# One normalisation a step earlier, its epsilon added column by column: a change to VectorE's order in a four-layer attention block

## The chip, the cores and the metric

One core of one Trainium2 chip runs the program. The time is the device time of one launch in microseconds, the median of three runs. The trace is one profiled execution of the same program, taken apart from those runs.

## The reference, cut to what matters

A batch of 16 sequences of 128 tokens with 128 features goes through four layers of cross attention and feed-forward, and then through one gated block of self attention and mixture of experts. The change touches the four layers alone.

```python
def _norm(x):
    m = jnp.mean(x, axis=-1, keepdims=True)
    s = jnp.sqrt(jnp.mean((x - m) ** 2, axis=-1, keepdims=True))
    return (x - m) / (s + EPS)                  # EPS = 1e-6, added to the root

def _attention(x, src, dist, bias, Wq, Wk, Wv, Wo, Wth, bth, Wto, bto):   # 16 heads of 64
    q = einsum('bfd,dnh->bfnh', x, Wq) * H ** (-0.5)
    k, v = einsum('btd,dnh->btnh', src, Wk), einsum('btd,dnh->btnh', src, Wv)
    hbias = relu(dist[..., None] @ Wth + bth)   # 32 values for each pair of positions
    qs_bias = (hbias @ Wto + bto)[..., 0]
    logits = einsum('btnh,bfnh->bnft', k, q) + bias + qs_bias[:, None]
    out = einsum('bnft,btnh->bfnh', softmax(logits), v)
    return einsum('bfnh,nhd->bfd', out, Wo)

for i in range(4):
    x = x + _attention(_norm(x), ctx, dist, mask, Wq[i], ...)     # first norm
    x = x + relu(_norm(x) @ Wf1[i] + bf1[i]) @ Wf2[i] + bf2[i]    # second norm
```

## The kernel before, in words

All data are float32 and stay in SBUF. One batch of one layer is a *unit*; there are 64 units, and unit u is batch u mod 16 of layer u div 16. A software pipeline goes through steps i = 0 to 63 (with -1 and 64 at the edges). In step i TensorE computes scores of unit i, applies the probabilities of unit i-1 and projects them out, makes keys, values and queries of unit i+1, the first feed-forward matmul of unit i-1 and the second of unit i-2. Each engine has its own hand-written order for a step, with semaphores between the engines; nothing reorders it at run time.

A unit is normalised twice: before its queries (half `a`, buffer half 0) and before its feed-forward (half `b`, half 1). Before the change, step i treats the *pair* of unit i+1's `a` and unit i-1's `b`. The way of such a pair is:

- VectorE: `residual1` (line 929) adds the projected attention of unit i-1; `stats` (881) and `moments` (886) make mean and variance of both halves.
- GpSimd: `root` (1317) raises both variances to 0.5 in one instruction, `sd`, a tile of 128x2.
- VectorE: `inverse_deviation` adds epsilon to both columns (891, `sde`) and takes the reciprocal (893, `rs`); `normalise` (900) writes `hh`, 128x128, once for `a` and once for `b`.
- TensorE: `turn_pair` transposes the two halves of `hh` (480 for `a`, 483 for `b`) into one PSUM bank; VectorE's `keep_pair` (909) copies both to `hhT`.
- TensorE: queries (427 on `hhT`) of unit i+1 and first feed-forward matmul (504) of unit i-1, after which ScalarE keeps the queries (709) and VectorE the hidden layer (942, `hid`).

TensorE's `turn_pair` stands behind the transposes of the first two quarters of the probabilities (406) and ahead of keys, queries and feed-forward of the step.

The bias of the scores, 32 relu terms for each of four units, is work that is spread over the steps as filler. ScalarE makes 22 relus (682), VectorE weighs and adds them (844; the first term of a group is 841) in PSUM, GpSimd makes the other ten terms with three instructions each on 128x512 (1333, 1340, 1352). `Z_PLAN`, `TERM_PLAN` and `POOL_PLAN` say how many go at each place of a step, by i mod 4; `more(q)` in VectorE's step runs the q-th entry of its plan. In the step that is 3 mod 4, VectorE ends with the sum of the two parts (852). GpSimd also multiplies the exponentials by the reciprocal sums (`norm`, 1321), four times a step, the third right behind `root`.

The stretch after the four layers (the gated block) has its own order. Its first pieces for two batches, `f_first` in 12 parts, run inside steps 61 and 62 at the places of `more`.

Of the kernel before, what the change touches and what calls it, by code (L numbers as in the profile page):

```python
# [8 lines left out]
ALU = mybir.AluOpType  # L9
# [33 lines left out]
TERM_PLAN = ((1, 1, 3, 1), (1, 1, 3, 1), (1, 1, 2, 1), (1, 1, 2, 1))  # L43
# [7 lines left out]
F_FIRST_PARTS = ((0, 1), (2, 3, 4, 5, 6), (7, 8, 9), (10, 11))  # L51
# [13 lines left out]
def wait(eng, sem, value):  # L65

    if value < 1:
        return
    eng.wait_ge(sem, value)
# [30 lines left out]
def block_program(nc, x, ctx_in, dist, mask, g_xattn, g_ffn, Wq, Wk, Wv, Wo, Wth, bth, Wto, bto,  # L100
                  Wf1, bf1, Wf2, bf2, W_qkv, b_qkv, W_gate, b_gate, W_experts, b_experts, out):
    with ExitStack() as stack:
# [3 lines left out]
        def sem(name):  # L106
            return stack.enter_context(nc.semaphore(name))
# [123 lines left out]
        bna, bnb, vara, varb, rooted, sdeps, rstd = [sem(n) for n in ("bna", "bnb", "vara", "varb", "rooted", "sdeps", "rstd")]  # L231
# [21 lines left out]
        def there(u):  # L253
            return 0 <= u < UNITS
# [4 lines left out]
        def pairs(i):  # L259

            return i + 2

        def halves(i):

            return slice(0 if there(i + 1) else 1, 2 if there(i - 1) else 1)

# [555 lines left out]
        def _(dve):  # L822
# [43 lines left out]
            def inverse(u, c):  # L866
                dve.wait_ge(exp_done, upto(u, 4, c))
                wait(dve, normed, upto(u - 1, 4, c))
                vec.reciprocal(rinv[:, c, :], rsum[:, c, :]).then_inc(inv_done, 1)  # L869

            def stats(u, a):

                s, b = u % 2, u % BATCHES
                if a == 1:
                    dve.wait_ge(resid1, upto(u))
                elif u < BATCHES:
                    dve.wait_ge(ln_done, b + 1)
                else:
                    dve.wait_ge(resid2, upto(u - BATCHES))
                wait(dve, hb_done if a else ha_done, upto(u - 2))  # L880
                vec.bn_stats(st[:, s, a, :], x_all[:, b, :]).then_inc(bnb if a else bna, 1)  # L881

            def moments(u, a):
                s = u % 2
                dve.wait_ge(bnb if a else bna, upto(u))
                vec.bn_aggr(mv[:, s, a, :], st[:, s, a, :]).then_inc(varb if a else vara, 1)

            def inverse_deviation(i):
                s, h = (i + 1) % 2, halves(i)
                dve.wait_ge(rooted, pairs(i))  # L890
                vec.tensor_scalar(sde[:, s, h], sd[:, s, h], NORM_EPS, None, ALU.add).then_inc(sdeps, 1)  # L891
                dve.wait_ge(sdeps, pairs(i))
                vec.reciprocal(rs[:, s, h], sde[:, s, h]).then_inc(rstd, 1)

            def normalise(u, a):
                s, b = u % 2, u % BATCHES
                i = u + 1 if a else u - 1
                dve.wait_ge(rstd, pairs(i))
                wait(dve, hh_done, pairs(i - 2))
                vec.tensor_scalar(hh[:, s, a, :], x_all[:, b, :], mv[:, s, a, 0:1], rs[:, s, a:a + 1],  # L900
                                  ALU.subtract, ALU.mult).then_inc(hb_done if a else ha_done, 1)
# [29 lines left out]
            def residual2(u):  # L931
                dve.wait_ge(f2_done, upto(u))
                dve.wait_ge(xb_done, upto(u))
                vec.tensor_tensor(x_all[:, u % BATCHES, :], FF_BANK[:, 0:P], xb[:, u % 2, :], ALU.add).then_inc(resid2, 1)
# [16 lines left out]
            def step(i):  # L951
# [3 lines left out]
                def more(q):  # L955

                    if i in F_EARLY:
                        for part in F_FIRST_PARTS[q]:
                            f_first(0, F_EARLY.index(i), part)
                    elif cur:  # L960
                        terms(plan[q])
# [13 lines left out]
                if cur:  # L975
                    inverse(i, 1)
                if prev:
                    residual1(i - 1)
                if nxt:
                    stats(i + 1, 0)  # L980
                if prev:
                    stats(i - 1, 1)
                if nxt:
                    moments(i + 1, 0)
                if prev:
                    moments(i - 1, 1)
                if cur:
                    inverse(i, 2)
                inverse_deviation(i)
                if nxt:  # L990
                    normalise(i + 1, 0)
                if prev:
                    normalise(i - 1, 1)
                more(1)
                if old:
                    residual2(i - 2)
                keep_pair(i)
# [8 lines left out]
                more(2)  # L1006
                if prev:
                    hidden(i - 1)
                more(3)
# [256 lines left out]
            stats(0, 0)  # L1266
            moments(0, 0)
            terms(2)
            keep_keys(0, 0)
            inverse_deviation(-1)  # L1270
            normalise(0, 0)
            terms(2)
            keep_pair(-1)
# [28 lines left out]
        def _(pool):  # L1302
# [7 lines left out]
            def root(i):  # L1310
                s, h = (i + 1) % 2, halves(i)
                if there(i + 1):
                    pool.wait_ge(vara, upto(i + 1))
                if there(i - 1):
                    pool.wait_ge(varb, upto(i - 1))
                wait(pool, sdeps, pairs(i - 2))
                gp.tensor_tensor(sd[:, s, h], mv[:, s, h, 1], half[:, 0:h.stop - h.start], ALU.pow).then_inc(rooted, 1)  # L1317
# [113 lines left out]
            ops(3)  # L1431
            root(-1)
# [31 lines left out]
```

## Time and profile before

| | |
|---|---|
| median of three runs | 1273.55 us (1273.51 to 1273.87) |
| profiled execution: its time | 1273.89 us |
| profiled execution: its span, first to last instruction | 1272.1 us |
| mean granted TensorE clock | 0.988 of full speed (2.4 GHz) |
| busy: TensorE matmul, VectorE, ScalarE, GpSimd | 91%, 87%, 84%, 63% of the span |

The first scores begin 38.4 us into the span and the last step's at 1075.9 us, so that the 64 steps are most of the time. Line numbers are those of the kernel before. In a timeline, a bracket shows how long the engine had been idle before the instruction, and which instruction ended that wait.

### The profile page before, as it was taken

What the parts mean: (1) busy time and instruction counts of PE and PEld (TensorE: products, weight loads), DVE (VectorE), ACT (ScalarE), POOL (GpSimd) and SP (SyncE); (2) the same over time, 40 slices, a digit from 0 to 9 for tenths busy, and PEclk for the clock granted to TensorE, in tenths of its full rate; (3) what the DMA queues carried; (4) which work ended last, traced back from release to release, by engine and by line L of the source; (5) the groups of instructions that cost most, each with busy time, mean ns of one, the idle gap of its engine ahead of it and who ended that gap; (6) DMA issues with size and microseconds to landing.
All of it is one profiled execution on the core that took longest, in us unless ns stands there. A gap on an engine that the chain in (4) does not pass through costs nothing.

```text
span 1272.1 us, 35758 instructions
## 1 busy us (share of the span) xinstructions
PE 1155.1 (91%) x11216; PEld 989.3 (78%) x11216; DVE 1103.9 (87%) x4455; ACT 1070.1 (84%) x3387; POOL 804.0 (63%) x917
## 2 busy tenths in 40 slices
PE   1499999999999999999999999999999999899897
PEld 1478888888888888888888888888888888666665
DVE  4988888888988888889898989898989887599996
ACT  4698888888888888888898888888888876588886
POOL 5577777777777777777777777777777733211110
PEclk9799999999999999999999999999999999899999
DMA  7400000001100000011000000000000000000000
GB/s 221 117 2 2 2 2 2 2 2 53 32 2 2 2 2 2 2 51 35 2 2 2 2 2 2 2 2 2 2 2 2 2 2 2 1 7 9 9 9 10
DMA packets 21147, 19.29 MB, mean 15 GB/s; under 512 B 5848, under 2 KB 17504, under 8 KB 20960
## 3 DMA queue, kind: packets, MB, share of 16 engines
q1 hardware_dynamic: 20960, 17.00, 4.5%
q8 instruction: 92, 1.51, 0.5%
q14 instruction: 95, 0.78, 0.2%
HBM read 15.95 MB, written 1.05 MB: 13 GB/s over the span
## 4 chain that ended last, share of the span: by engine, by line
PE 57%; DVE 25%; issue 8%; POOL 4%; ACT 3%; SPq 1%; DMA 1%; DVEq 0%; POOLq 0%; ACTq 0%
PE B L427 13%; PE B L392 10%; PE B L420 9%; PE B L469 9%; DVE B L844 6%; DVE sde L891 5%; DVE hh L900 4%; POOL sd L1317 3%; PE B L567 3%; PE B L406 2%; PE B L504 2%; ACT prob L753 2%; PE B L579 2%; PE B L646 2%; DVE st L881 2%
## 5 line engine op out<-in xcount | busy, mean ns | idle before, releaser
L1321 POOL TENSOR_TENSOR prob<-prob,rinv 128x512 f32<-128x512 f32 x256 | 266.6, 1041 | 266.8 <-DVE rinv L869 264.4
L692 ACT ACTIVATE prob<-score,nmax 128x128 f32<-128x128 f32 x1024 | 395.4, 390 | 9.6 <-DVE nmax L861 7.5
L682 ACT ACTIVATE relu_z<-dist_all,cst_all 128x512 f32<-128x512 f32 x356 | 276.6, 811 | 12.1 <-DMA dist_all<-in_fside_BxSxS 10.5
L861 DVE CUSTOM_DVE_ANT_0 score<-B,bias 128x128 f32<-128x128 f32 x1024 | 225.0, 284 | 42.8 <-PE B L392 42.7
L844 DVE SCALAR_TENSOR_TENSOR B<-relu_z,cst_all,B 128x512 f32<-128x512 f32 x340 | 254.4, 748 | 6.8 <-ACT relu_z L682 2.6
L692 ACT ACTIVATION_READ_ACCUMULATOR prob<-score,nmax 128x1 f32 x1024 | 194.4, 190 | 0.0
L709 ACT ACTIVATE qT<-B 128x512 f32<-128x512 f32 x128 | 76.7, 599 | 128.1 <-PE B L427 128.1
L1352 POOL TENSOR_TENSOR pool_acc<-pool_acc,clamped 128x512 f32<-128x512 f32 x140 | 178.3, 1273 | 6.7
L427 PE MATMUL B<-ctxT_all,wk 128*128 128x128 f32 x1024 | 143.5, 284 | 14.8 <-DVE nmax L861 14.1
L427 PEld LDWEIGHTS B<-ctxT_all,wk 128*128 128x128 f32 x1024 | 129.4, 197 | 25.8 <-DVE nmax L861 14.3
L406 PEld LDWEIGHTS B<-ident,prob 128*128 128x128 f32 x1024 | 120.2, 141 | 35.6 <-issue 33.4
L699 ACT ACTIVATE probT<-B 128x512 f32<-128x512 f32 x256 | 141.7, 592 | 3.7 <-PE B L406 3.6
L427 PE MATMUL B<-hhT,wq 128*128 128x128 f32 x1024 | 142.4, 283 | 1.8 <-DVE hhT L909 0.9
L406 PE MATMUL B<-ident,prob 128*128 128x128 f32 x1024 | 143.1, 273 | 0.6 <-POOL prob L1321 0.6
L392 PE MATMUL B<-kT,qT 64*128 64x128 f32 x2048 | 131.5, 278 | 11.3 <-DVE hid L942 10.5
L392 PEld LDWEIGHTS B<-kT,qT 64*128 64x128 f32 x2048 | 120.2, 188 | 23.2 <-issue 23.2
L427 PEld LDWEIGHTS B<-hhT,wq 128*128 128x128 f32 x1024 | 125.6, 193 | 11.4 <-DVE hhT L909 10.7
L449 PE MATMUL B<-wv,ctxT_all 128*128 128x512 f32 x256 | 131.5, 596 | 0.0
L1340 POOL TENSOR_SCALAR clamped<-clamp_in,cst_all 128x512 f32<-128x512 f32 x156 | 123.0, 788 | 11.0
L1333 POOL TENSOR_SCALAR clamp_in<-dist_all,cst_all 128x512 f32<-128x512 f32 x156 | 121.6, 779 | 9.5 <-DVE cst_all L1244 9.5
L469 PE MATMUL B<-wo,oT 128*128 128x128 f32 x1024 | 125.2, 275 | 1.8 <-issue 1.8
L420 PE MATMUL B<-probT,v 128*64 128x128 f32 x2048 | 125.9, 276 | 0.0
(135 smaller groups left out, 2110.4 us busy)
## 6 DMA issues: line engine op xcount, KB each, us to landing
wk<-in_L_xattn_Wk SPq DMA_DIRECT2D x4, 512.0 KB, 4.5
wv<-in_L_xattn_Wv SPq DMA_DIRECT2D x4, 512.0 KB, 5.6
wq<-in_L_xattn_Wq SPq DMA_DIRECT2D x4, 512.0 KB, 5.6
wo<-in_L_xattn_Wo SPq DMA_DIRECT2D x4, 512.0 KB, 6.2
wf<-in_L_xattn_Wf SPq DMA_DIRECT2D x8, 256.0 KB, 5.0
out<-outF SPq DMA_DIRECT2D x16, 64.0 KB, 1.5
dist_all<-in_fside_BxSxS SPq DMA_DIRECT2D x1, 768.0 KB, 9.4
mask_all<-in_mask_Bx1x1xS_ff SPq DMA_DIRECT2D x1, 768.0 KB, 10.9
```

The lines of the kernel that those rows point to most:

```text
L392: last = mm(S_BANK[2 * octet + r][:, m * P:(m + 1) * P], qT[64 * r:64 * r + 64, s, j, :], kT[64 * r:64 * r + 64, s, j, :], start=True, sto ...
L406: last = nc.tensor.transpose(T_BANK[c][:, m * P:(m + 1) * P], prob[:, c, m, :], ident[:, :])
L420: last = mm(O_BANK[octet][64 * r:64 * r + 64, m * P:(m + 1) * P], v[:, u % 2, n * HD:(n + 1) * HD], probT[:, 2 * octet + r, m * P:(m + 1) ...
L427: last = mm(dst[:, m * P:(m + 1) * P], w[:, j * P:(j + 1) * P], src, start=True, stop=True)
L469: last = mm(WO_BANK[:, 0:P], oT[:, u % 2, j, :], wo[:, slot_of(u), j, :], start=j == 0, stop=j == PAIRS - 1)
L682: nc.scalar.activation(relu_z[:, j % Z_SLOTS, :], bias_flat(dist_all, g), ACT.Relu, bias=cst_all[:, l, C_BTH + k:C_BTH + k + 1], scale=cst ...
L692: last = nc.scalar.activation(prob[:, c, m, :], score[:, c, m, :], ACT.Exp, bias=nmax[:, c, m:m + 1], scale=-1.0, accum_out=rsum[:, c, m:m ...
L699: nc.scalar.activation(probT[:, c, :], T_BANK[c][:, :], copy).then_inc(pT_kept, 1)
L844: vec.scalar_tensor_tensor(out=ACC[:, :], in0=relu_z[:, j % Z_SLOTS, :], scalar=weight, in1=ACC[:, :], op0=ALU.mult, op1=ALU.add).then_inc ...
L861: last = vec.tensor_tensor_reduce(out=score[:, c, m, :], in0=S_BANK[c][:, m * P:(m + 1) * P], in1=bias[:, u // GROUP % 2, u % GROUP, :], s ...
L1321: gp.tensor_tensor(prob[:, c, :, :], prob[:, c, :, :], rinv[:, c, :].rearrange("p (m o) -> p m o", o=1).broadcast_to([P, 4, P]), ALU.mult) ...
L1352: gp.tensor_tensor(pool_acc[:, g % 2, :], so_far, clamped[:, :], ALU.add).then_inc(pool_sum, 1)
```

## The change

Unit i+2's `a` takes the place of unit i+1's in the pair that step i roots and inverts: its statistics, its root, its epsilon and its reciprocal are made with unit i-1's `b`, and its `normalise` stands near the end of the step, one step ahead of the transposition that reads it. The transposed pair stays unit i+1's `a` and unit i-1's `b`. Epsilon is added by two instructions on one column each, with a semaphore for each (`epsa`, `epsb` in place of `sdeps`); the reciprocal stays one instruction on both columns. Of VectorE's bias terms, one moves ahead of `inverse_deviation` (it stood behind `normalise`); of those that stood together behind the keys, one goes between `residual2` and `keep_pair` in the steps that are 0 and 1 mod 4, and one goes behind `hidden`. Before the first step, units 0 and 1 are both normalised, with a `root` each. GpSimd's order is otherwise the same; `root` waits for its own later readers by the two new semaphores. The parts of `f_first` are laid on the six places anew.

```diff
-TERM_PLAN = ((1, 1, 3, 1), (1, 1, 3, 1), (1, 1, 2, 1), (1, 1, 2, 1))
+TERM_PLAN = ((1, 1, 1, 1, 1, 1), (1, 1, 1, 1, 1, 1), (1, 1, 0, 1, 1, 1), (1, 1, 0, 1, 1, 1))
-F_FIRST_PARTS = ((0, 1), (2, 3, 4, 5, 6), (7, 8, 9), (10, 11))
+F_FIRST_PARTS = ((0, 1), (), (2, 3, 4, 5, 6), (7, 8), (9,), (10, 11))
...
             def inverse_deviation(i):
-                s, h = (i + 1) % 2, halves(i)
-                dve.wait_ge(rooted, pairs(i))
-                vec.tensor_scalar(sde[:, s, h], sd[:, s, h], NORM_EPS, None, ALU.add).then_inc(sdeps, 1)
-                dve.wait_ge(sdeps, pairs(i))
+                s, h = i % 2, root_halves(i)
+                dve.wait_ge(rooted, roots(i))
+                if there(i + 2):
+                    vec.tensor_scalar(sde[:, s, 0:1], sd[:, s, 0:1], NORM_EPS, None, ALU.add).then_inc(epsa, 1)
+                if there(i - 1):
+                    vec.tensor_scalar(sde[:, s, 1:2], sd[:, s, 1:2], NORM_EPS, None, ALU.add).then_inc(epsb, 1)
+                if there(i + 2):
+                    dve.wait_ge(epsa, upto(i + 2))
+                if there(i - 1):
+                    dve.wait_ge(epsb, upto(i - 1))
                 vec.reciprocal(rs[:, s, h], sde[:, s, h]).then_inc(rstd, 1)
...
                 if cur:
                     inverse(i, 1)
+                if there(i + 2):
+                    stats(i + 2, 0)
                 if prev:
                     residual1(i - 1)
-                if nxt:
-                    stats(i + 1, 0)
+                if there(i + 2):
+                    moments(i + 2, 0)
                 if prev:
                     stats(i - 1, 1)
-                if nxt:
-                    moments(i + 1, 0)
-                if prev:
                     moments(i - 1, 1)
                 if cur:
                     inverse(i, 2)
-                inverse_deviation(i)
-                if nxt:
-                    normalise(i + 1, 0)
+                more(1)
+                if there(i + 2) or prev:
+                    inverse_deviation(i)
                 if prev:
                     normalise(i - 1, 1)
-                more(1)
                 if old:
                     residual2(i - 2)
+                more(2)
                 keep_pair(i)
...
                     keep_keys(i + 1, 1)
-                more(2)
+                more(3)
                 if prev:
                     hidden(i - 1)
-                more(3)
+                more(4)
+                if there(i + 2):
+                    normalise(i + 2, 0)
+                more(5)
...
             def root(i):
-                s, h = (i + 1) % 2, halves(i)
-                if there(i + 1):
-                    pool.wait_ge(vara, upto(i + 1))
+                s, h = i % 2, root_halves(i)
+                if there(i + 2):
+                    pool.wait_ge(vara, upto(i + 2))
                 if there(i - 1):
                     pool.wait_ge(varb, upto(i - 1))
-                wait(pool, sdeps, pairs(i - 2))
+                wait(pool, epsa, min(upto(i), UNITS))
+                wait(pool, epsb, upto(i - 3))
...
+            root(-2)
             root(-1)
```

## Rows read from the trace of the kernel before

**Rows 1.** The page's chain of work that ended last: shares of the span by line.

```profile
PE B L427 13%; PE B L392 10%; PE B L420 9%; PE B L469 9%; DVE B L844 6%; DVE sde L891 5%; DVE hh L900 4%; POOL sd L1317 3%; PE B L567 3%; PE B L406 2%; PE B L504 2%; ACT prob L753 2%; PE B L579 2%; PE B L646 2%; DVE st L881 2%
```

**Rows 2.** The waits: who waited for whom, us in total, times, longest.

```profile
PE B L480 <- DVE hh L900: 29.1, 56, 4.9
...
PE B L483 <- DVE hh L900: 14.7, 16, 1.5
```

**Rows 3.** Windows of four steps, steps 1 to 59, step 60: length, engines' busy time.

```profile
core 0: us, PE busy (x) PEld busy (x) DVE busy (x) ACT busy (x) POOL busy (x), PEclk, DMA share, GB/s
605.09:621.26 16.17, 15.41 (x150) 13.53 (x150) 14.43 (x58) 14.19 (x46) 12.41 (x14) 1.00 0.01 2
621.26:636.96 15.70, 15.41 (x152) 13.53 (x151) 13.65 (x58) 14.02 (x46) 11.74 (x14) 1.00 0.01 2
636.96:654.19 17.23, 15.62 (x152) 13.55 (x151) 15.85 (x60) 14.49 (x47) 12.29 (x14) 1.00 0.01 2
654.19:670.32 16.13, 15.47 (x150) 13.55 (x151) 14.35 (x59) 14.64 (x47) 12.53 (x15) 1.00 0.01 2
65.61:1028.41 962.80, 914.70 (x8867) 801.05 (x8866) 858.91 (x3410) 845.18 (x2685) 720.17 (x794) 1.00 0.02 7
1028.41:1043.65 15.24, 15.18 (x151) 13.46 (x150) 11.33 (x54) 10.59 (x41) 5.25 (x6) 1.00 0.01 2
```

**Rows 4.** Timeline of TensorE in step 60, which has no bias terms.

```profile
1036.83 0.60 PE L406 MATMUL B<-ident,prob 128*128 128x128 f32 x4
1037.26 1.02 PE L449 MATMUL B<-wv,ctxT_all 128*128 128x512 f32 x2
1038.12 0.60 PE L406 MATMUL B<-ident,prob 128*128 128x128 f32 x4
1038.78 0.30 PE L480 MATMUL B<-ident,hh 128*128 128x128 f32 x1
```

**Rows 5.** Timeline of VectorE in the step from 605.09: start, duration, instruction.

```profile
606.25 0.29 DVE L861 CUSTOM_DVE_ANT_0 score<-B,bias 128x128 f32<-128x128 f32 x1 [0.65 <-PE B L392]
...
613.73 1.00 DVE L891 TENSOR_SCALAR sde<-sd 128x2 f32<-128x2 f32 x1 [0.76 <-POOL sd L1317]
...
614.97 1.31 DVE L900 TENSOR_SCALAR hh<-x_all,mv,rs 128x128 f32<-128x128 f32 x2
```

**Rows 6.** Timeline of GpSimd in the same step.

```profile
613.67 1.04 POOL L1321 TENSOR_TENSOR prob<-prob,rinv 128x512 f32<-128x512 f32 x1
614.66 1.27 POOL L1352 TENSOR_TENSOR pool_acc<-pool_acc,clamped 128x512 f32<-128x512 f32 x1
```

**Rows 7.** Timeline of TensorE in the same step.

```profile
609.97 1.95 PE L469 MATMUL B<-wo,oT 128*128 128x128 f32 x16
...
616.16 0.30 PE L480 MATMUL B<-ident,hh 128*128 128x128 f32 x1 [0.76 <-DVE hh L900]
```

**Rows 8.** Timelines of VectorE and GpSimd in step 0, which roots one column.

```profile
60.35 0.15 DVE L891 TENSOR_SCALAR sde<-sd 128x1 f32<-128x1 f32 x1 [0.94 <-POOL sd L1317]
...
60.28 1.04 POOL L1321 TENSOR_TENSOR prob<-prob,rinv 128x512 f32<-128x512 f32 x1
```

**Rows 9.** All `hh`; the page's group of the terms; VectorE in step 60.

```profile
L900 DVE TENSOR_SCALAR hh<-x_all,mv,rs x128: 333/572/1443, 31.4 to 1096.8; 128x128 f32<-128x128 f32 x128
...
L844 DVE SCALAR_TENSOR_TENSOR B<-relu_z,cst_all,B 128x512 f32<-128x512 f32 x340 | 254.4, 748 | 6.8 <-ACT relu_z L682 2.6
...
1042.00 0.69 DVE L942 TENSOR_TENSOR hid<-B,nb_all 128x512 f32<-128x512 f32 x1 [1.00 <-PE B L504]
```

**Rows 10.** ScalarE and TensorE at 469: in step 1 (from 65.61), in step 63.

```profile
69.95 0.58 ACT L714 ACTIVATE oT<-B 128x512 f32<-128x512 f32 x1
...
70.94 1.24 PE L469 MATMUL B<-wo,oT 128*128 128x128 f32 x9 [0.29 <-issue]
...
1079.89 0.60 ACT L714 ACTIVATE oT<-B 128x512 f32<-128x512 f32 x1 [0.19 <-PE B L420]
...
1080.59 0.68 PE L469 MATMUL B<-wo,oT 128*128 128x128 f32 x4 [0.74 <-issue]
```

More of the change, by code:

```diff
@@ L230, in block_program @@
         pool_mul, pool_clamp, pool_sum = sem("pool_mul"), sem("pool_clamp"), sem("pool_sum")
-        bna, bnb, vara, varb, rooted, sdeps, rstd = [sem(n) for n in ("bna", "bnb", "vara", "varb", "rooted", "sdeps", "rstd")]
+        bna, bnb, vara, varb, rooted, epsa, epsb, rstd = [sem(n) for n in ("bna", "bnb", "vara", "varb", "rooted", "epsa", "epsb", "rstd")]
         ha_done, hb_done, hh_done, hh_kept = [sem(n) for n in ("ha_done", "hb_done", "hh_done", "hh_kept")]
@@ L265, in halves, with roots, root_halves @@
             return slice(0 if there(i + 1) else 1, 2 if there(i - 1) else 1)
+        def roots(i):
+            return i + 3
+        def root_halves(i):
+            return slice(0 if there(i + 2) else 1, 2 if there(i - 1) else 1)
         def bias_flat(tile, g):
@@ L869, in inverse, with root_slot @@
                 vec.reciprocal(rinv[:, c, :], rsum[:, c, :]).then_inc(inv_done, 1)
+            def root_slot(u, a):
+                return (u + 1 if a else u - 2) % 2
             def stats(u, a):
-                s, b = u % 2, u % BATCHES
+                s, b = root_slot(u, a), u % BATCHES
                 if a == 1:
@@ L883, in moments @@
             def moments(u, a):
-                s = u % 2
+                s = root_slot(u, a)
                 dve.wait_ge(bnb if a else bna, upto(u))
@@ L888, in inverse_deviation @@
             def inverse_deviation(i):
-                s, h = (i + 1) % 2, halves(i)
-                dve.wait_ge(rooted, pairs(i))
-                vec.tensor_scalar(sde[:, s, h], sd[:, s, h], NORM_EPS, None, ALU.add).then_inc(sdeps, 1)
-                dve.wait_ge(sdeps, pairs(i))
+                s, h = i % 2, root_halves(i)
[8 more added lines that the diff above has]
+                    dve.wait_ge(epsb, upto(i - 1))
                 vec.reciprocal(rs[:, s, h], sde[:, s, h]).then_inc(rstd, 1)
             def normalise(u, a):
[L896 to L900, printed above, removed]
+                s, b = root_slot(u, a), u % BATCHES
+                dve.wait_ge(rstd, roots(u + 1 if a else u - 2))
+                wait(dve, hh_done, pairs(u - 1 if a else u - 3))
+                vec.tensor_scalar(hh[:, u % 2, a, :], x_all[:, b, :], mv[:, s, a, 0:1], rs[:, s, a:a + 1],
                                   ALU.subtract, ALU.mult).then_inc(hb_done if a else ha_done, 1)
@@ L1266, in _ @@
             stats(0, 0)
+            stats(1, 0)
             moments(0, 0)
+            moments(1, 0)
             terms(2)
             keep_keys(0, 0)
-            inverse_deviation(-1)
+            inverse_deviation(-2)
             normalise(0, 0)
             terms(2)
+            inverse_deviation(-1)
+            normalise(1, 0)
             keep_pair(-1)
```

## The prediction, made before the changed kernel ran

> **What bounds the kernel now.** I read the chain of waits first, because it names the work that sets the end. TensorE's matmuls head it, but three small things follow them closely: epsilon (891) with 5% of the span, `hh` (900) with 4% and GpSimd's root (1317) with 3% [rows 1]. They work on tiles of 128x2 or 128x128, and all lie on the way from `residual1` to the transposition of `hh`. The view of waits says what that way costs TensorE: 29.1 + 14.7 us of idling at the two transpositions [rows 2].
>
> The windows show how this is spread. Four steps in a row take 16.17, 15.70, 17.23 and 16.13 us, 65.23 together, and the pattern repeats; they are the steps 2, 3, 0 and 1 mod 4. TensorE is busy 15.4 to 15.6 us in each. ScalarE has 14.0 to 14.6 and GpSimd less; VectorE has 13.7 to 14.4, and 15.85 in one step, in which its busy time holds a long `hh` [rows 3]. What differs from step to step is how long TensorE waits. So the bound is TensorE plus one chain that passes over VectorE and GpSimd once a step.
>
> **How long a step is without that wait.** Step 60, without bias work, takes 15.24 us [rows 3]. Its first four transpositions start 0.43 us before what follows them (1036.83 to 1037.26), its second four 0.66 us before 480 (1038.12 to 1038.78) [rows 4]: 0.23 is still a wait for `hh`. That leaves 15.24 - 0.23 = 15.01 us. The same rows show why waits cost more than their idle time: an instruction that waits for nothing starts 0.17 us ahead of the modelled end of the one before (1036.83 + 0.60 = 1037.43 against 1037.26), and this overlap is lost as well. So the 962.80 - 914.70 = 48.1 us that TensorE is idle in steps 1 to 59 [rows 3] is less than what can be won there.
>
> **What the change does to the chain**, in the step from 605.09.
>
> *Before.* VectorE idles 0.76 us for the root. Epsilon on 128x2 then takes 1.00 us, to 614.73 [rows 5]. GpSimd's multiplication (1321) ends at 614.71 [rows 6]: the addition ended when that did. `hh` starts at 614.97, behind a GpSimd instruction that ends at 615.93, and its two halves, 0.33 us each when free [rows 9], are done at 616.28 [rows 5, 6]. TensorE has waited 0.76 us, since 615.40 [rows 7].
>
> *Epsilon by columns.* In step 0 the root has one column, and there the addition takes 0.15 us with GpSimd's 1321 running all around it [rows 8]. A 128x1 addition does not wait for GpSimd; two cost at most 0.30 in place of 1.00.
> The Trainium skill's "Perfetto Trace Analysis", section "Optimizing Scalar/DVE Operations", speaks against splitting: each VectorE instruction pays about 60 ns of access to SBUF anew. By it some 60 added instructions would cost an estimated 3.6 us if nothing covered them. The 0.15 us of the row is no smaller than that; the cover follows.
>
> *The `b` half.* The root ends at 613.7. Two additions and the 0.24 us between epsilon and `hh` [rows 5] put `normalise` of `b` at about 614.3, under 1321. It then waits for the end of 1321, as epsilon did, and ends within 0.1 us of it, at 614.8, where it was 616.28. Without waiting TensorE would start 480 at 615.40 - 0.17 = 615.23 and 483, which reads `b`, after it: a slack of about 0.5 us. So the waits of [rows 2] go. The added instruction is covered by 1321; without that cover it costs 60 x 0.15 = 9 us at most.
>
> *Terms.* One term (0.75 us [rows 9]) goes into the 0.76 us in front of epsilon. One goes ahead of `keep_pair` in two steps of four, where VectorE would otherwise wait for the transpositions. Their number stays.
>
> *The `a` half.* Its statistics fill time in which VectorE waits for TensorE's 469, its root shares the old instruction. Its `normalise` meets GpSimd's bias work at the end of the step and takes 0.33 us if free, up to 1.44 if not [rows 9]. In step 60 `hid` starts 1042.00 - 1028.41 = 13.59 us into the step, after waiting for TensorE [rows 3, 9]; without the 0.23, at 13.36. After it come 0.7 for itself, a term, `hh`, a term: done at 15.9 to 17.0, and 0.7 later in the steps 3 mod 4, which end with the bias sum. The next scores can start 15.01 + 1.16 = 16.17 us into the step, as they started 1.16 after 605.09 [rows 5]. So VectorE is on time in three steps of four or nearly so, and 0.4 to 1.5 late in the fourth. The slack of 0.5 at `b` and some 0.2 ahead of `residual1` absorb 0.7. I take 0.2 us in each of the 15 steps 3 mod 4, 3 us. Bounds: nothing, and 0.8 in these 15, 12 us.
>
> *What is late next: ScalarE.* In the steps 0 and 1 mod 4 it ends with three relus, and the next step's exponentials and `oT` stand behind them. Until now TensorE's own waits hid that. In step 1, which began without such a wait, `oT` is kept at 70.53, 4.92 us into the step, and 469, which reads it, starts at 5.33 instead of 609.97 - 605.09 = 4.88 [rows 7, 10]. There it waits for the layer's weights too; in step 63, which does not, it starts 0.10 after `oT` (1080.49 to 1080.59) [rows 10], which would be 5.02. So the 30 steps 1 and 2 mod 4 are longer by 0.14 to 0.45. I take 0.2, near the second row, since most steps load no weights: 15.21 us.
>
> **The sum.** From 65.61 to 1028.41 lie steps 1 to 59, 962.80 us [rows 3]. After the change: 30 steps of 15.21, 456.3; 29 of 15.01, 435.3; the three that open a layer hold eight matmuls more (492), at 15.41 / 150 [rows 3] each 0.1, 2.4; and 3 for the late scores. Together 897.0, a gain of 65.8. Step 60 gives 0.2. Ahead of the loop VectorE is behind, and it gets one more normalisation: between nothing (some of it falls into waits for relus) and 1.44 + 0.15 + 0.24 = 1.8; I take 1.0. The last steps and the gated block I leave as they are. 65.8 + 0.2 - 1.0 = 65.0. The profiled execution would go from a span of 1272.1 to 1207.1, and with the 1.8 us around it from 1273.89 to 1208.9; the median lies 0.3 below that, 1273.55 - 65.0 = 1208.55, say **1208.5 us**.
>
> **Rivals.**
> 1. *ScalarE holds 469 up as in step 1.* It was the same instruction behind the same relus [rows 10]; against it only the four waits there. 30 x 0.25 = 7.5 more: 1216 us. Chance 0.15.
> 2. *`hh` loses its turn against GpSimd.* When 1321 ends, GpSimd's next instruction might be served before the waiting `b`. Against it: epsilon, waiting just so, ended with 1321 and not 1.27 us later [rows 5, 6]. For it: an `hh` of 1.44 us, more than the rest of any one GpSimd instruction [rows 6, 9]. Then `b` is 0.8 to 1.3 late against a slack of 0.5, or the moved `a` exceeds the 0.7 absorbed. At 0.2 to 0.6 us in 59 steps 12 to 35 us come back, 1220 to 1244, most likely 1228. Chance 0.17.
> The Trainium skill's "SBUF — State Buffer", section "Who interferes with whom", calls it a lock between GpSimd and VectorE's two-port mode: "Whoever issues first gets the shared pair for the whole instruction; the other **fully blocks**". By it the waiting `b` goes ahead of GpSimd's next, and the moved `a` stands behind one in progress. The 1.00 us of epsilon agrees with it.
> 3. *The change doesn't do what it says: one column waits for GpSimd too.* Step 0 speaks against it [rows 8]. `b` would start where `hh` starts now and end with the next GpSimd instruction, 0.1 to 0.7 us after TensorE wants it; at 0.3 in 59 steps, 1226. Chance 0.03.
> 4. *Slower: VectorE becomes the bound,* by the moved `normalise` at the step's end. A step now takes 962.80 / 59 = 16.32 us on average. In the step from 654.19 VectorE is busy 14.35 [rows 3]; less 0.7 for epsilon and less the moved `hh` it needs about 13.2, with short waits 13.6. The moved `hh` would have to take more than 2.7 us in every step; its longest is 1.44. At 3.2 the time is 1273.55 + 59 x 0.5 = 1303. Chance 0.03.
>
> **How the numbers follow.** The forecast (1202 to 1214) has 0.62. With rival 1 and the nearer half of rival 2 and 3, 1199 to 1232 holds some 0.85; the bounds of the late scores (-3, +9), of 469 (-2, +7.5) and of the start (-0.8, +1) lie in it. Less than 0.2%, 2.5 us, this kernel's measurements cannot tell from no change. Faster: all but rival 4 and a rival 2 of twice its price: 0.95. Same 0.02, slower 0.03.
>
> **What would show it.** Right: 891 at 150 ns, twice a step; no wait at 480 and 483; short waits at 469 in the steps 1 and 2 mod 4; steps near 15.0 and 15.2; VectorE waiting for TensorE at `hid`. Wrong: a `b` half that ends with the second GpSimd instruction after the root; TensorE waiting at 469 in all steps (late scores) or at 427 behind `hhT`; 891 still near 1 us.

## The result, and the profile after

The change makes the kernel faster: 1201.18 us, median of four runs (1201.02 to 1201.37), against 1273.53 for the kernel before on the same chip; the ratio is 0.9434, with a 95% interval of 0.9417 to 0.945. The forecast was 1208.5 us, so 65.0 us of gain were expected and 72.4 came. The time lies 0.8 us below the narrower range of the prediction, 1202 to 1214 (chance 0.62), and inside its wider one, 1199 to 1232 (0.85).

The windows of the profile after, by stage: steps 1 to 59, and what follows step 62 (steps 60 to 62 lie between the two and take 45.97 us). Below them stand four steps in a row (20 to 23, which are 0, 1, 2 and 3 mod 4) and the step that opens the second layer (16). The columns are those of [rows 3].

```profile
65.43:955.54 890.11, 889.34 (x8867) 797.55 (x8866) 806.66 (x3468) 834.98 (x2685) 714.45 (x794) 1.00 0.03 8
1001.51:1199.30 197.79, 170.98 (x1755) 127.75 (x1754) 160.89 (x722) 155.11 (x504) 28.77 (x52) 0.97 0.03 7
...
352.17:367.07 14.90, 14.90 (x151) 13.44 (x150) 14.15 (x60) 13.90 (x46) 11.48 (x13) 1.00 0.01 2
367.07:382.21 15.14, 15.14 (x151) 13.52 (x150) 13.86 (x61) 14.39 (x47) 12.79 (x16) 1.00 0.01 2
382.21:397.36 15.15, 15.15 (x152) 13.52 (x151) 13.10 (x58) 14.40 (x47) 12.21 (x14) 1.00 0.01 2
397.36:412.27 14.91, 14.91 (x152) 13.45 (x152) 13.62 (x60) 13.91 (x46) 12.08 (x15) 1.00 0.01 2
...
290.87:306.82 15.95, 15.95 (x159) 14.41 (x159) 14.46 (x61) 14.01 (x46) 11.91 (x14) 1.00 0.16 46
```

Beside [rows 3]: steps 1 to 59 take 890.11 us in place of 962.80, and that is the whole gain (72.7 of 72.8 us of span). In them TensorE is busy 889.34 of 890.11 us. The pattern of four has gone from 65.23 us to 60.10; the steps 0 and 3 mod 4 are equal now, the other two 0.23 longer. What lies before step 1 and behind step 59 has changed by 0.1 us in all.

The page's chain that ended last says the same, and so do the waits (some rows of the whole run: who waited for whom, us in total, times, longest):

```profile
PE B L434 20%; PE B L399 10%; PE B L476 10%; PE B L427 10%; PE B L413 9%; PE B L456 9%; PE B L511 5%; PE B L521 4%; PE B L574 3%; PE B L653 3%; ACT prob L760 3%; PE B L586 3%; DVE B L851 1%; DMA score<-in_ctx 1%; PE B L642 1%
```

```profile
DVE hid L959 <- PE B L511: 23.2, 64, 1.2
DVE score L868 <- PE B L399: 18.3, 43, 0.9
...
DVE sde L904 <- POOL sd L1341: 4.2, 18, 0.7
```

Where epsilon, `hh` and the root had 12% of the span in [rows 1], none of them is among the lines that the page shows any more; the root, as the largest, has 0.2% left. The 29.1 and 14.7 us of [rows 2] are down to 1.8 and 2.7 us, all but 0.2 of it outside steps 1 to 59; now VectorE waits for TensorE, at `hid` and at the scores. (Lines have moved: 392 is 399 after the change, 427 is 434, 469 is 476, 480 and 483 are 487 and 490, 891 is 904 and 906, 900 is 917, 1317 and 1321 are 1341 and 1345.)

The heart of the change in one step (the one from 352.17, beside [rows 5 to 7]): timelines of VectorE, GpSimd and TensorE.

```profile
360.95 0.15 DVE L904 TENSOR_SCALAR sde<-sd 128x1 f32<-128x1 f32 x1 [0.15 <-POOL sd L1341]
361.02 0.14 DVE L906 TENSOR_SCALAR sde<-sd 128x1 f32<-128x1 f32 x1
361.26 0.17 DVE L911 RECIPROCAL rs<-sde 128x2 f32<-128x2 f32 x1
361.46 0.54 DVE L917 TENSOR_SCALAR hh<-x_all,mv,rs 128x128 f32<-128x128 f32 x1
```

```profile
360.89 1.04 POOL L1345 TENSOR_TENSOR prob<-prob,rinv 128x512 f32<-128x512 f32 x1
```

```profile
362.32 0.27 PE L487 MATMUL B<-ident,hh 128*128 128x128 f32 x1
362.43 0.27 PE L490 MATMUL B<-ident,hh 128*128 128x128 f32 x1
362.53 1.06 PE L434 MATMUL B<-ctxT_all,wk 128*128 128x128 f32 x8
```

Both additions are over at 361.16, while 1345 runs until 361.93. `hh` for `b` is issued at 361.46 under 1345 and ends at 362.00, 0.07 after it. TensorE wants `b` at 362.43: 0.43 us to spare, where 0.5 had been forecast. The two transpositions follow each other at 0.11 us, without a wait.

### The profile page after: what moved, and what is told of

Read it like the earlier page. It is cut to its first block, busy times and chain, and to the rows that moved or that the text cites. A ratio compares the mean times of both kernels' runs of the same rounds, so it can differ in the third digit from the quotient of the medians.

```text
span 1199.3 us, 35943 instructions
## 1 busy us (share of the span) xinstructions
PE 1134.4 (95%) x11216; PEld 988.7 (82%) x11216; DVE 1050.9 (88%) x4518; ACT 1060.1 (88%) x3387; POOL 798.7 (67%) x918
## 3 DMA queue, kind: packets, MB, share of 16 engines
HBM read 15.95 MB, written 1.05 MB: 14 GB/s over the span
## 4 chain that ended last, share of the span: by engine, by line
PE 88%; ACT 4%; DVE 3%; issue 2%; SPq 1%; DMA 1%; POOL 0%; ACTq 0%; DVEq 0%; POOLq 0%
PE B L434 20%; PE B L399 10%; PE B L476 10%; PE B L427 10%; PE B L413 9%; PE B L456 9%; PE B L511 5%; PE B L521 4%; PE B L574 3%; PE B L653 3%; ACT prob L760 3%; PE B L586 3%; DVE B L851 1%; DMA score<-in_ctx 1%; PE B L642 1%
## 5 line engine op out<-in xcount | busy, mean ns | idle before, releaser
L689 ACT ACTIVATE relu_z<-dist_all,cst_all 128x512 f32<-128x512 f32 x356 | 279.9, 821 | 11.3 <-DMA dist_all<-in_fside_BxSxS 10.1
L699 ACT ACTIVATION_READ_ACCUMULATOR prob<-score,nmax 128x1 f32 x1024 | 206.4, 202 | 0.0
L434 PEld LDWEIGHTS B<-ctxT_all,wk 128*128 128x128 f32 x1024 | 125.9, 194 | 23.9 <-DVE nmax L868 12.2
L434 PE MATMUL B<-hhT,wq 128*128 128x128 f32 x1024 | 137.4, 278 | 1.9 <-DVE hhT L926 1.9
L456 PE MATMUL B<-wv,ctxT_all 128*128 128x512 f32 x256 | 134.0, 607 | 0.0
L1364 POOL TENSOR_SCALAR clamped<-clamp_in,cst_all 128x512 f32<-128x512 f32 x156 | 120.0, 769 | 11.0
```

What stands on the lines that cost most here:

```text
L434: last = mm(dst[:, m * P:(m + 1) * P], w[:, j * P:(j + 1) * P], src, start=True, stop=True)
L456: mm(V_BANK[a][:, :], ctxT_all[:, u % BATCHES, :], wv[:, slot_of(u), a * 512:(a + 1) * 512], start=True, stop=True).then_inc(v_done, 1)
L689: nc.scalar.activation(relu_z[:, j % Z_SLOTS, :], bias_flat(dist_all, g), ACT.Relu, bias=cst_all[:, l, C_BTH + k:C_BTH + k + 1], scale=cst ...
L699: last = nc.scalar.activation(prob[:, c, m, :], score[:, c, m, :], ACT.Exp, bias=nmax[:, c, m:m + 1], scale=-1.0, accum_out=rsum[:, c, m:m ...
```

## The experiments

All times are medians, with the ratio to the kernel before as measured beside them. "Steps 1 to 59" is from each profile's windows; two profiles of one kernel agree there within 0.6 us, while the end of the program varies by more (last experiment).

| Kernel | us | ratio, 95% interval | steps 1 to 59, us |
|---|---|---|---|
| before | 1273.5 to 1275.5 | 1 | 962.80 |
| after | 1201.18 | 0.9434 (0.9417 to 0.945) | 890.11 |
| order alone, one epsilon (e1) | 1230.74 | 0.9656 (0.9638 to 0.9675) | 920.31 |
| split alone, old order (e2) | 1226.0 | 0.9618 (0.9597 to 0.9638) | 913.69 |
| term put back (e3) | 1217.63 | 0.9546 (0.9528 to 0.9565) | 906.39 |
| term put back, later (e3b) | 1204.51 | 0.944 (0.9415 to 0.9465) | 894.23 |
| even relus (e4) | 1192.66 | 0.9362 (0.9343 to 0.9381) | 882.93 |
| even relus in the kernel before (e4b) | 1273.99 | 0.9998 (0.9985 to 1.001) | 962.34 |
| moved half done twice (e5) | 1208.58 | 0.9473 (0.9449 to 0.9497) | 895.89 |
| epsilon from a tile (e6) | 1234.14 | 0.9686 (0.9661 to 0.9711) | 921.29 |

### The order without the split, and the split without the order

The order alone (e1): the changed kernel with one epsilon on both columns.

```diff
-                if there(i + 2):
-                    vec.tensor_scalar(sde[:, s, 0:1], sd[:, s, 0:1], NORM_EPS, None, ALU.add).then_inc(epsa, 1)
-                if there(i - 1):
-                    vec.tensor_scalar(sde[:, s, 1:2], sd[:, s, 1:2], NORM_EPS, None, ALU.add).then_inc(epsb, 1)
...
+                vec.tensor_scalar(sde[:, s, h], sd[:, s, h], NORM_EPS, None, ALU.add).then_inc(sdeps, 1)
```

> The changed kernel with epsilon added by one instruction on both columns again; everything else as changed. Theory (a two-column addition waits for GpSimd's multiplication behind the root, a one-column addition does not): the addition takes 1.0 us again, the reciprocal ends near 9.8 us into the step, and normalise of b, which starts then, meets the next GpSimd instruction and ends with it, 0.3 to 1.1 us after TensorE wants it at 10.1; 0.55 us in each of 59 steps come back, about 1233 us (1220 to 1240). Rival (the new order has made the chain slack, so that the length of epsilon no longer matters): within 4 us of the changed kernel, 1197 to 1205 us.

Measured 1230.74 us. VectorE, GpSimd and TensorE in one of the worst steps (2 mod 4, from 392.83):

```profile
401.71 1.00 DVE L903 TENSOR_SCALAR sde<-sd 128x2 f32<-128x2 f32 x1
...
402.95 1.05 DVE L911 TENSOR_SCALAR hh<-x_all,mv,rs 128x128 f32<-128x128 f32 x1
```

```profile
401.65 1.04 POOL L1338 TENSOR_TENSOR prob<-prob,rinv 128x512 f32<-128x512 f32 x1
402.65 1.27 POOL L1369 TENSOR_TENSOR pool_acc<-pool_acc,clamped 128x512 f32<-128x512 f32 x1
```

```profile
404.05 0.33 PE L490 MATMUL B<-ident,hh 128*128 128x128 f32 x1 [0.58 <-DVE hh L911]
```

Epsilon on two columns ends with GpSimd's first instruction (402.71 and 402.69), `b` with its second (404.00 and 403.92). That second wait is what the split saves. Where a 0.77 us instruction follows on GpSimd (steps 0 and 1 mod 4), `b` costs TensorE 0.21 and 0.10 us of recorded idling; where one of 1.27 follows, 0.58. The steps 0, 1, 2 and 3 mod 4 are longer than in the changed kernel by more than that, 0.66, 0.53, 0.78 and 0.23 us: the overlap in front of 490 is lost as well, and in the steps 0 and 1 mod 4 the first two matmuls of the queries on `hhT` come another 0.12 and 0.10 later. In e1 the moved `normalise` and the moved terms stand together; no run moves the half alone.

The split alone (e2): the same two additions in the order of the kernel before.

```diff
-                vec.tensor_scalar(sde[:, s, h], sd[:, s, h], NORM_EPS, None, ALU.add).then_inc(sdeps, 1)
...
+                if there(i + 1):
+                    vec.tensor_scalar(sde[:, s, 0:1], sd[:, s, 0:1], NORM_EPS, None, ALU.add).then_inc(epsa, 1)
+                if there(i - 1):
+                    vec.tensor_scalar(sde[:, s, 1:2], sd[:, s, 1:2], NORM_EPS, None, ALU.add).then_inc(epsb, 1)
```

> The kernel before with epsilon added one column at a time and nothing else changed. Theory (the split takes VectorE's addition out of the wait for GpSimd, and the order gives the rest): the addition takes 0.15 us, the a half of hh ends with GpSimd's multiplication near 9.7 us into the step, the b half follows at once or one GpSimd instruction later, and TensorE's wait for hid at the start of two steps of four stays; steps of 15.2 to 15.6 us, 1213 to 1228 us. Rival (the moved normalisation is what counts, the split little): 1250 to 1274 us. Rival (the split is all): 1197 to 1205 us.

Measured 1226.0 us. Its pair of `hh` in two steps, from 375.24 and from 390.62, the instructions of GpSimd around them, and TensorE:

```profile
384.40 0.79 DVE L906 TENSOR_SCALAR hh<-x_all,mv,rs 128x128 f32<-128x128 f32 x2
...
399.78 1.77 DVE L906 TENSOR_SCALAR hh<-x_all,mv,rs 128x128 f32<-128x128 f32 x2
```

```profile
383.81 1.04 POOL L1328 TENSOR_TENSOR prob<-prob,rinv 128x512 f32<-128x512 f32 x1
384.84 0.83 POOL L1340 TENSOR_SCALAR clamp_in<-dist_all,cst_all 128x512 f32<-128x512 f32 x1
...
399.20 1.04 POOL L1328 TENSOR_TENSOR prob<-prob,rinv 128x512 f32<-128x512 f32 x1
400.20 1.27 POOL L1359 TENSOR_TENSOR pool_acc<-pool_acc,clamped 128x512 f32<-128x512 f32 x1
```

```profile
390.62 0.60 PE L392 MATMUL B<-kT,qT 64*128 64x128 f32 x6 [0.37 <-DVE hid L948]
...
401.61 0.33 PE L483 MATMUL B<-ident,hh 128*128 128x128 f32 x1 [0.56 <-DVE hh L906]
```

This is near what rival 2 feared, one instruction further back: not the half that waits loses its turn but the one behind it. Both halves are in line under 1328. In the first step both are through at 385.19, 0.34 after its end, and GpSimd's 1340 takes 0.83 in place of 0.77. In the second step the pair ends at 401.55, 0.08 after 1359: the second half has lost its turn, and TensorE waits 0.56 at 483. So in these rows a VectorE instruction that stands waiting goes ahead of GpSimd's next one; one that comes behind it may not. With one half in place of two, as after the change, there is nothing to lose: `b` ends 0.08 us after 1345 in 58 of the 59 steps. The Trainium skill's "SBUF — State Buffer", section "Who interferes with whom", says that issue order decides who blocks. These rows agree for the half that waits. The half behind it starts 0.02 to 0.04 us after GpSimd's next instruction in both steps; it is blocked in one, as by that rule, and not in the other.

The other cost left in e2 is the 0.37 at 392: `hid` ends late and TensorE's scores stand behind the feed-forward (row from 390.62). The kernel before had this wait too, in the steps 0 and 1 mod 4:

```profile
PE B L392 <- DVE hid L942: 10.5, 29, 0.4
```

e2 keeps it with the same three numbers; e1 and the changed kernel have none, so the order removes it. Together: 49.1 us of steps 1 to 59 for the split alone, 42.5 for the order alone, 72.7 for both. The two gains overlap by 18.9 us: either of them shortens the same way to the transposition of `b`.

### What the place of a term is worth

With two terms ahead of the copy of `hhT` and none ahead of epsilon (e3), and with none ahead of epsilon and the term behind the layer's keys (e3b), in the plan of terms:

```diff
-TERM_PLAN = ((1, 1, 1, 1, 1, 1), (1, 1, 1, 1, 1, 1), (1, 1, 0, 1, 1, 1), (1, 1, 0, 1, 1, 1))
+TERM_PLAN = ((1, 0, 2, 1, 1, 1), (1, 0, 2, 1, 1, 1), (1, 0, 1, 1, 1, 1), (1, 0, 1, 1, 1, 1))   # e3
+TERM_PLAN = ((1, 0, 1, 2, 1, 1), (1, 0, 1, 2, 1, 1), (1, 0, 0, 2, 1, 1), (1, 0, 0, 2, 1, 1))   # e3b
```

> The changed kernel with the bias term that stands ahead of epsilon put back behind normalise and residual2, ahead of keep_pair. Theory (the term's place counts where it delays hhT): VectorE idles for the root again, nothing changes up to b, and in the steps 0 and 1 mod 4, which then have two terms ahead of keep_pair, hhT ends some 0.7 us after TensorE wants it: 30 x 0.7 = 21 us, about 1222 us (1212 to 1228). In the steps 2 and 3 mod 4 nothing. Rival (VectorE has slack enough, the place of a term does not matter): within 3 us of the changed kernel, 1198 to 1204 us.

> The changed kernel with no term ahead of epsilon, but that term stands two places later than in the run before it (behind the copy of the layer's keys, in front of the hidden unit's second group), so that VectorE's order from the root to the copy of hhT is as short as it can be. Theory (a term ahead of epsilon falls into the wait for GpSimd's root and costs nothing; what cost 16 us in the run with the term put behind the copy of hhT's pair was its place there, in front of what TensorE waits for): VectorE idles some 0.7 us for the root, the b half is as early as now or earlier, the waits at L434 behind hhT are as now (under 0.1), and the time is 1201 to 1206. Rival (the term hides nothing that another place would not hide, so that any place but one is bad): the hidden unit gets later by one term, 0.75 us, TensorE waits for it at L399 in the steps where it has least to spare, and the time is 1210 to 1225.

Measured 1217.63 and 1204.51 us. In e3 the two terms stand in front of what TensorE wants next (step from 356.78, VectorE and TensorE):

```profile
366.73 1.53 DVE L851 SCALAR_TENSOR_TENSOR B<-relu_z,cst_all,B 128x512 f32<-128x512 f32 x2
368.17 0.42 DVE L926 COPY hhT<-B 128x256 f32<-128x256 f32 x1
```

```profile
368.64 0.82 PE L434 MATMUL B<-hhT,wq 128*128 128x128 f32 x5 [0.44 <-DVE hhT L926]
```

In e3b VectorE idles for the root, 45.0 us in all where it was 4.2, and no new wait shows in TensorE's list; the steps 0 mod 4 still take 15.20 in place of 14.91, and hardly any others differ. The cause is at their start. VectorE comes to them late by part of what it spent waiting, and there the bias sum (859) stands ahead of the scores. Their first instruction in the step from 353.77, then the same one in the changed kernel, step from 352.17:

```profile
355.57 0.29 DVE L868 CUSTOM_DVE_ANT_0 score<-B,bias 128x128 f32<-128x128 f32 x1
```

```profile
353.59 0.29 DVE L868 CUSTOM_DVE_ANT_0 score<-B,bias 128x128 f32<-128x128 f32 x1
```

The scores start 1.80 us into the step in place of 1.42. Behind them 476, which reads `oT`, starts 0.12 later and its next matmul another 0.07, and the second matmul of the queries on `hhT` 0.10 more: 0.29 without a recorded wait. So the term in the root's wait is worth 15 x 0.29 = 4.4 us (894.23 - 890.11 = 4.1), through the late scores behind the steps 3 mod 4 that the prediction had named; the expectation that nothing would be lost there was too good.

### The relus

Even relus in the changed kernel (e4) and in the kernel before (e4b):

```diff
-Z_PLAN = ((1, 1, 1, 3), (1, 1, 1, 3), (1, 1, 1, 2), (1, 1, 1, 2))
+Z_PLAN = ((1, 1, 2, 2), (1, 1, 2, 2), (1, 1, 1, 2), (1, 1, 1, 2))
```

> The changed kernel with one relu of ScalarE moved from the end of the steps 0 and 1 mod 4 to the place ahead of the queries, so that each step ends with two. Theory (the three relus at the end of a step hold up oT and with it 469 in the next): the 0.23 us that the steps 1 and 2 mod 4 are longer go, 30 x 0.23 = 6.9 us, 1194 us (1193 to 1197), and all steps take 14.9 us. Rival (469 waits for something else, or the moved relu delays the queries by as much): 1200 us or more.

> The kernel before with ScalarE's relus two and two in the last two slots of the steps 0 and 1 mod 4 (1, 1, 2, 2 in place of 1, 1, 1, 3); nothing else. Theory (the relus held 469 up in the kernel before as well, but TensorE's wait for the b half hid it, so the same edit that gave the changed kernel 8.5 us gives this one nothing or less than 3): 1270 to 1276. Rival (the gain of the even relus is independent of the change and is worth the same here): 1264 to 1268.

Measured 1192.66 and 1273.99 us. ScalarE and TensorE in a step 2 mod 4 of the changed kernel (from 382.21), and of e4 (from 379.88):

```profile
386.56 0.59 ACT L721 ACTIVATE oT<-B 128x512 f32<-128x512 f32 x1
...
387.25 1.02 PE L476 MATMUL B<-wo,oT 128*128 128x128 f32 x7
```

```profile
383.88 0.60 ACT L721 ACTIVATE oT<-B 128x512 f32<-128x512 f32 x1 [0.19 <-PE B L427]
...
384.76 0.50 PE L476 MATMUL B<-wo,oT 128*128 128x128 f32 x3
```

With three relus `oT` ends 4.94 us into the step and 476 starts at 5.04, 0.10 behind it. With two, ScalarE waits for TensorE instead, `oT` ends at 4.60 and 476 starts at 4.88. All steps then take 14.91 us, and steps 1 to 59 are 7.2 us shorter, which is 30 x 0.23 and a little. In the kernel before the same edit gives nothing: its four steps take 17.23, 16.13, 16.17 and 15.69 us with it and without. The time of e4 is 0.3 us below what was expected, since what follows step 62 took 196.2 us, and 197.8 in the changed kernel's profile (last section). e4 is faster than both kernels.

### Doing the moved half twice

The second time into a tile that nobody reads (e5).

```diff
+            def again(u):
...
+                vec.tensor_scalar(spare[:, :], x_all[:, b, :], mv[:, s, 0, 0:1], rs[:, s, 0:1],
+                                  ALU.subtract, ALU.mult).then_inc(spared, 1)
...
+                    again(i + 2)
```

> The changed kernel with the moved normalisation of the a half done twice in every step, the second time into a tile that nobody reads; everything else as it is. Measures how much room the end of VectorE's step has, which the prediction put at nothing (three steps of four) and 0.2 us lost in the fourth. By the changed kernel's trace the scores started up to 0.6 us late and TensorE did not wait. Theory (there is at least another 0.4 to 1.0 us of room, as the run with late scores of 1.63 us suggests): within 3 us of the changed kernel, 1200 to 1205. Rival (the room is used up, as the prediction took it): each of the steps 3 mod 4 loses 0.4 to 1.0 us, 15 of them 6 to 15 us, and the steps 0 mod 4 a part: 1207 to 1220, with waits at L434 or L399 that name VectorE.

Measured 1208.58 us, 5.8 us more in steps 1 to 59: the rival's time. But the loss is not where either theory had it. Steps 3 mod 4 keep their 14.91; steps 0 mod 4 take 15.10 and steps 1 mod 4 15.41 in place of 15.14. VectorE, ScalarE and TensorE at the start of one of the latter (from 428.70):

```profile
428.76 1.44 DVE L919 TENSOR_SCALAR hh<-x_all,mv,rs 128x128 f32<-128x128 f32 x1
...
430.77 0.28 DVE L870 CUSTOM_DVE_ANT_0 score<-B,bias 128x128 f32<-128x128 f32 x1
```

```profile
433.28 0.57 ACT L723 ACTIVATE oT<-B 128x512 f32<-128x512 f32 x1
```

```profile
433.95 0.46 PE L478 MATMUL B<-wo,oT 128*128 128x128 f32 x2 [0.21 <-DVE oT L950]
```

The scores start 2.07 us into the step; in the changed kernel they start at 1.20. The exponentials and `oT` follow them, and 478 waits. In the steps 0 mod 4 they start at 1.68 for 1.42. So late scores do cost, by way of `oT`, and in the steps 0 mod 4 the changed kernel has less than 0.26 us to spare.

### Epsilon from a tile

One addition on both columns with two inputs from SBUF (e6).

```diff
+                vec.tensor_tensor(sde[:, s, h], sd[:, s, h], epsc[:, 0:h.stop - h.start], ALU.add).then_inc(sdeps, 1)
```

> The changed kernel with epsilon added to both columns in one instruction, which has two inputs from SBUF (the deviations and a 128x2 tile that holds epsilon) in place of one input and a constant. Tells whether it is the count of two elements that made the addition end with GpSimd's multiplication, or the form with one input and a constant. Theory A (an addition on two columns waits for GpSimd in any form): 0.9 to 1.0 us per addition and the time of the run with one two-column epsilon, 1226 to 1233. Theory B (only the form with a constant waits): 0.1 to 0.2 us per addition, b as early as now, 1198 to 1203.

Measured 1234.14 us. VectorE and GpSimd:

```profile
371.06 1.00 DVE L905 TENSOR_TENSOR sde<-sd,epsc 128x2 f32<-128x2 f32 x1 [0.16 <-POOL sd L1338]
372.09 0.17 DVE L907 RECIPROCAL rs<-sde 128x2 f32<-128x2 f32 x1
```

```profile
371.00 1.04 POOL L1342 TENSOR_TENSOR prob<-prob,rinv 128x512 f32<-128x512 f32 x1
```

It ends with GpSimd's instruction, as the other form on two columns does (372.06 and 372.04), and the time is 1.1 us above theory A's range. But the run does not show that it is the count: in step 0, where the root has one column, this form waits as well, and there [rows 8] have 0.15 us with one input.

```profile
60.16 0.99 DVE L905 TENSOR_TENSOR sde<-sd,epsc 128x1 f32<-128x1 f32 x1 [0.28 <-POOL sd L1338]
```

```profile
60.09 1.04 POOL L1342 TENSOR_TENSOR prob<-prob,rinv 128x512 f32<-128x512 f32 x1
```

For the form with one input the count does decide beside the multiplication: two columns took 1.00 us in 60 of 62 in the kernel before (0.17 in the other two, beside a GpSimd instruction on 128x1), one column 0.14 to 0.16 in all 128 in the changed kernel. Why, no run here shows. The section "Who interferes with whom" of the Trainium skill's "SBUF — State Buffer" says that a VectorE instruction with two inputs from SBUF contends with a GpSimd instruction that reads SBUF. 63 of e6's 67 additions agree: they end with GpSimd's instruction. The other four, two of them beside GpSimd's 1354 and 1361, which read SBUF too, took 0.15 to 0.16 us, and do not. The reciprocal on the same two columns, issued as GpSimd starts its next instruction, takes 0.17.

### The last stretch, again

The changed kernel and e4 once more, without an edit.

> The changed kernel once more, without an edit. In its first profile TensorE's granted clock fell to 0.50 for some 5 us about 12 us before the end, and the stretch from the last transposition of hF to the end took 30.30 us in place of 26.94. Theory (the fall belongs to a single execution: whether TensorE's idle time in the gated block is met by a lower clock differs from one execution to the next): steps 1 to 59 again 890.1 us within 0.3, and the last stretch at another length between 26.9 and 30.3. Rival (the fall belongs to the changed kernel): the last stretch again 30.3 us with the clock at 0.50.

> The changed kernel with the even relus once more, without an edit. In its first profile the last stretch took 26.99 us at a clock of 1.00. Theory (single execution): steps 1 to 59 again 883.3 us within 0.5; the last stretch may be anything from 26.9 to 30.3. Rival (the fall hangs on the kernel): again 27.0 us at 1.00. Under both the time is 1191 to 1196, below the changed kernel's 1201, since at most 3.4 us of the 8.5 between them can be the clock at the end.

Measured 1199.68 us (ratio 0.9424, 0.9406 to 0.9442) and 1193.38 us (0.9371, 0.9352 to 0.9389). Steps 1 to 59 took 889.56 and 882.90 us, within 0.6 of the first time (0.3 had been expected for the changed kernel). The stretch from the last transposition of `hF` to the end took 28.58 and 26.98 us, where the first profiles had 30.30 and 26.99.

## Why the prediction was right, and what was mis-sized

The mechanisms were all there: epsilon at 0.15 and 0.14 us, `b` ending with GpSimd's first instruction, no wait at the transpositions, VectorE waiting for TensorE at `hid`, two kinds of steps set apart by three relus. One wait was missing from the account: TensorE's 10.5 us at 392 for `hid`, which the sum counts as gone, by starting from a step that has none, without saying what would end it; the order did. Of the rivals none came true: 469 costs the sum's price and not the first rival's, and `b` never lost its turn in steps 1 to 59. The forecast was 7.3 us too high, just past its narrower range; its terms were off by 11.4 us one way and 3.6 the other, so that part of the nearness is luck. The terms of the sum, against the profile's 72.8 us of span:

- **A step without waits: 15.01 taken, 14.91 measured.** The working started from step 60, took off its recorded wait of 0.23 [rows 4], and stopped there. The transpositions behind that wait, in the trace of before, still follow each other at 0.17:

```profile
1038.95 0.33 PE L483 MATMUL B<-ident,hh 128*128 128x128 f32 x1
1039.12 1.06 PE L427 MATMUL B<-ctxT_all,wk 128*128 128x128 f32 x8
```

  After the change they follow at 0.11 and 0.10 (362.32, 362.43, 362.53). The prediction had itself said that a wait loses the overlap behind it, and then did not apply this to the two instructions that come next. 59 x 0.10 = 5.9 us.
- **469 behind the relus: 0.20 taken, 0.23 measured;** e4 confirms place and size. -0.9 us.
- **The steps that open a layer: 0.8 taken above the others, 1.04 measured** (15.95), and the steps behind them 0.16 more. -1.2 us.
- **Late scores: 3 us taken, none measured in the steps named.** `hh` takes 0.34 to 1.40 us, as taken, but the step's end had more room: even after a moved half of 1.00 us, in the step from 382.21, the scores of the next start at 1.19. In the steps 0 mod 4 they start at 1.42, and the step keeps its 14.91. Behind the steps that open a layer, where the moved half takes 1.40 us, they start at 1.58; these are the steps that are 0.16 longer, and how much of that is theirs no run shows. e5 shows that the room is small: one more `hh` a step costs 5.8 us. +3 us. These four make 6.8 of the 6.9 by which steps 1 to 59 (890.1) are shorter than forecast (897.0).
- **The start: 1.0 us later taken, 0.2 earlier measured** (65.43 for 65.61). The profiles of the changed kernel's other versions lie between 64.97 and 65.79, so no cost can be seen there. +1.2 us.
- **Steps 60 to 62: 0.2 taken, 1.5 gained.** Steps 61 and 62 hold the same wait for `b`, and the prediction left them out. +1.3 us.
- **The rest: 1.5 us longer** (197.79 for 196.26). Up to the last transposition of `hF` it is 1.8 shorter, behind it 3.3 longer (30.30 for 26.99); in both parts the profile with the longer time at a granted clock of 0.50 is the longer one (below).

6.9 + 1.2 + 1.3 - 1.5 = 7.9, which is the 72.8 less the 65.0 of the forecast, but for rounding.

The prediction gave the Trainium skill's rule that each VectorE instruction pays its access anew ("Perfetto Trace Analysis", "Optimizing Scalar/DVE Operations") as a possible 3.6 us against the split. The Trainium skill says this there for an engine that is saturated, and adds that breaking up instructions may get work done sooner where VectorE is not saturated but causes bubbles on other engines. Here VectorE was busy 87% of the span, TensorE waited for it, and the split paid. The cover that the prediction named, GpSimd's multiplication (now 1345), holds: both additions end 0.77 us before it.

## What to carry to other kernels

Where two engines hold each other up, count which instructions stand in line: here an instruction that waited got through when the other engine's current one ended, and a chain of two such instructions paid twice. Making the first of them small enough not to wait (49.1 us), and taking one of the two `hh` behind it out of the chain (42.5, with the terms moved beside it), each brought most of the 72.7; they must not be added up. When an idle time is taken out of a step, apply the regained overlap to every instruction behind it, and look at the next engine in the row (here three relus on ScalarE): an edit that was worth nothing before was then worth 7 us.

## What was not expected of the hardware

Near the end of the gated block the granted clock of TensorE fell in some executions and not in others. Here are a window in the changed kernel's first profile, and the one with the lowest clock in its second (the granted clock is the third number from the end):

```profile
1184.00:1189.00 5.00, 5.00 (x22) 3.72 (x21) 1.59 (x4) 2.67 (x9) 0.00 (x0) 0.50 0.00 0
```

```profile
1181.80:1186.80 5.00, 4.52 (x27) 3.77 (x28) 1.63 (x4) 3.13 (x12) 0.00 (x0) 0.66 0.00 0
```

A clock of 0.50 is the lower of the two levels, 1.2 GHz. The four large matmuls (653) of that place show it (TensorE in the first profile of the changed kernel, then in the second of e4, where the clock was at 1.00 there):

```profile
1183.06 1.98 PE L574 MATMUL B<-kF,qm 32*128 32x128 f32 x16 [0.99 <-ACT prob L760]
...
1186.93 3.43 PE L653 MATMUL B<-we,hFT 128*128 128x512 f32 x4
```

```profile
1179.38 1.16 PE L574 MATMUL B<-kF,qm 32*128 32x128 f32 x16 [0.98 <-ACT prob L760]
...
1181.51 1.88 PE L653 MATMUL B<-we,hFT 128*128 128x512 f32 x4
```

Ahead of both TensorE had waited the same time for ScalarE, 0.99 and 0.98 us. In one execution the clock fell behind this wait, in the other it did not, and the same kernel showed two outcomes (30.30 and 28.58 us for the last stretch, with the clock at 0.50 for some 7 and some 3 us).

It fell earlier in the block too, in every profile, and there also for different times. In the second profile of e4:

```profile
1016.80:1030.50 13.70, 12.80 (x57) 8.97 (x57) 7.45 (x32) 7.04 (x25) 1.10 (x2) 0.50 0.00 0
```

In the changed kernel's two profiles this lower stretch is some 3 us long, in the kernel before some 10. From the end of step 62 to the last transposition of `hF` they take 167.5 and 167.4 us, the kernel before 169.3 and e4's second 170.7. So up to 3.3 us hang on the first fall and up to 3.3 on the second, each 0.3% of the time; over all profiles what follows step 62 takes 196.0 to 199.4 us. What decides it no run here shows; the steps of the four layers, where TensorE now has hardly a gap, are at 1.00 throughout, as they were before.
